# VectorE makes the low halves of the attention's x ahead of the FFN's output addition, and tiles 4 to 7 share one series of inverse deviations

## What is computed

```
def _layernorm(x, axis=-1, eps=1e-05):
    m = jnp.mean(x, axis=axis, keepdims=True)
    v = jnp.var(x, axis=axis, keepdims=True)
    return (x - m) / jnp.sqrt(v + eps)
...
    x = x + 0.5 * _L0_ffn_ref(_layernorm(x, axis=-1), ...)
    x = x + _L0_attn_ref(_layernorm(x, axis=-1), ...)
    x = x + 0.5 * _L0_ffn_ref(_layernorm(x, axis=-1), ...)
```

## Time and profile before

| | |
|---|---|
| median of 3 runs | 733.87 us (733.69 to 734.22) |
| the profiled execution | 733.68 us |
| its span, first to last instruction | 732.0 us |
| PE busy | 713.9 us (98%) |
| DVE, ACT, POOL busy | 523.8, 422.3, 400.6 us (72, 58, 55%) |

### The profile page before, as it was taken

One profiled execution on the slowest core, in us unless ns is written; L12 is line 12 of the kernel. 1 busy time (PEld: TensorE's weight loads), 2 busy tenths in 40 slices (PEclk: granted clock), 3 DMA queues, 4 the chain that ended last, 5 costly groups with the idle time before them and its releaser, 6 DMA issues.

```text
span 732.0 us, 13725 instructions
## 1 busy us (share of the span) xinstructions
PE 713.9 (98%) x3692; PEld 601.6 (82%) x3692; DVE 523.8 (72%) x1773; ACT 422.3 (58%) x1144; POOL 400.6 (55%) x503
## 2 busy tenths in 40 slices
PE   8998989999999999999999999999999999999998
PEld 6786768888888888888888888888888888878776
DVE  6769676767776777677776777667767777778675
ACT  3455675556664775567655765576556665655330
POOL 2566676535853486447743865277535853473420
PEclk9999999999999999999999999999999999999999
DMA  8140003000310022002200220012000300030002
GB/s 268 50 173 30 0 27 105 14 1 2 104 42 2 0 84 59 1 1 72 72 0 1 68 61 15 1 48 82 15 1 13 103 14 1 0 117 1 1 30 87
DMA packets 25868, 32.33 MB, mean 44 GB/s; under 512 B 5833, under 2 KB 14281, under 8 KB 25298
## 3 DMA queue, kind: packets, MB, share of 16 engines
q1 hardware_dynamic: 25232, 30.69, 13.3%
q10 hardware_dynamic: 578, 1.05, 0.4%
HBM read 27.54 MB, written 4.19 MB: 43 GB/s over the span
## 4 chain that ended last, share of the span: by engine, by line
PE 85%; DVE 7%; POOL 4%; ACT 2%; issue 1%; DMA 1%; SPq 0%; DVEq 0%; ACTq 0%; POOLq 0%
PE bank L1157 33%; PE bank L1215 23%; PE bank L1200 8%; PE bank L1179 7%; PE bank L1123 4%; PE bank L1187 4%; PE bank L1176 2%; POOL wo_lo L387 1%; DVE stats L762 1%; PE bank L1166 1%; PE bank L1177 1%; DVE xnT_lo L785 1%; PE bank L1140 1%; DMA x<-in_L_attn_x 1%; PE bank L1108 1%
## 5 line engine op out<-in xcount | busy, mean ns | idle before, releaser
L395 POOL TENSOR_TENSOR swap<-swap,rope 128x512 f32<-128x512 f32 x80 | 104.8, 1309 | 112.2 <-ACT swap L567 112.0
L402 POOL TENSOR_SCALAR_AFFINE_SELECT pT_hi_lo<-pT_hi_lo 128x256 fp32r<-128x256 f32 x128 | 51.9, 406 | 146.1 <-DVE pT_hi_lo L915 146.1
L593 ACT ACTIVATE bank<-sm,nmax 128x128 f32<-128x128 f32 x128 | 47.6, 372 | 111.0 <-DVE nmax L900 110.8
L567 ACT ACTIVATE swap<-bank 64x512 f32<-64x512 f32 x160 | 94.8, 593 | 12.7 <-PE bank L1157 10.2
L601 ACT ACTIVATE pT_hi_lo<-bank 128x256 fp32r<-128x256 f32 x128 | 49.0, 383 | 91.4 <-PE bank L1187 63.0
L915 DVE TENSOR_TENSOR pT_hi_lo<-bank,pT_hi_lo 128x256 fp32r<-128x256 f32 x128 | 53.6, 419 | 50.2 <-ACT pT_hi_lo L601 50.1
L412 POOL TENSOR_TENSOR q_lo<-rot,q_hi 128x512 fp32r<-128x512 f32 x64 | 82.6, 1290 | 1.6 <-ACT q_hi L575 1.6
L1215 PE MATMUL bank<-wo_hi,oT_hi 128*128 128x512 f32 x256 | 74.6, 413 | 0.3 <-DVE x L928 0.3
L1157 PE MATMUL bank<-xnT_lo,wq_hi 128*128 128x512 f32 x256 | 73.3, 390 | 0.0
L1157 PE MATMUL bank<-xnT_hi,wq_hi 128*128 128x512 f32 x256 | 71.9, 393 | 0.8 <-DVE v_lo L886 0.8
L1157 PE MATMUL bank<-xnT_hi,wq_lo 128*128 128x512 f32 x256 | 72.2, 394 | 0.0
(11 more groups left out here) (152 smaller groups left out, 1696.0 us busy)
## 6 DMA issues: line engine op xcount, KB each, us to landing
raw<-in_L_attn_wq SPq DMA_DIRECT2D x32, 256.0 KB, 3.0
raw<-in_L_attn_wo SPq DMA_DIRECT2D x32, 256.0 KB, 2.6
x<-in_L_attn_x SPq DMA_DIRECT2D x4, 512.0 KB, 7.4
raw<-in_L_attn_wk SPq DMA_DIRECT2D x8, 256.0 KB, 2.7
raw<-in_L_attn_wv SPq DMA_DIRECT2D x8, 256.0 KB, 3.5
out<-x SPq DMA_DIRECT2D x8, 256.0 KB, 2.0
raw<-in_L_ffn_W_base ACTq DMA_DIRECT2D x4, 256.0 KB, 5.4
wb_keep_hi<-q_hi SPq DMA_DIRECT2D x1, 1024.0 KB, 5.0
```

What stands on the lines that cost most here:

```text
L395: nc.gpsimd.tensor_tensor(w, w, tab, ALU.mult).then_inc(t2_done, 1)
L402: nc.gpsimd.affine_select(pT_both[:, :, 2, h, :], pT_both[:, :, 1, h, :].bitcast(F32), pattern=[[0, 2], [1, P]], compare_op=ALU.is_ge, fil ...
L567: last = nc.scalar.activation(swap[a:a + half, m % 2, :], A[m % 2][b:b + half, :], ACT.Copy)
```

## The change

VectorE's list: after the last `router`, `x_lo` of tiles 0 and 1 goes ahead of `ffn_out(0, 2)`, and `ht_lo(0, 3)` and `x_lo` of tiles 2 and 3 go ahead of the statistics of tile 5. The deviations of tiles 4 to 7 come from one series on VectorE, four columns wide, with the cosines of the key put between its first and second Newton step. GpSimd's series for tiles 4 and 5 goes (17 rows of its list, `shift` and the guess included), and one `split_lo` moves behind two bias additions. ScalarE's list: two swapped copies before it waits for the series, and all four `xn` of tiles 4 to 7 after. TensorE projects 36 products before it transposes tiles 4 and 5, 12 more before tiles 6 and 7, and puts the first scores ahead of the value pass. No data and no shapes change beyond that.

```diff
@@ rstd_steps @@
-            for _ in range(NEWTON):
+            for n in range(NEWTON):
+                if n == 1 and amid is not None:
+                    amid()
@@ gpsimd @@
             bias(0, 5)
-            split_lo(KT, KT % RING, wq_s[0][:, KT - 1, :], wq_s[1][:, KT - 1, :])
             bias(0, 6)
             bias(0, 7)
-            norm_rstd(1, 4, 6)
+            split_lo(KT, KT % RING, wq_s[0][:, KT - 1, :], wq_s[1][:, KT - 1, :])
             split_lo(5, 0, wv_s[0][:, :, :], wv_s[1][:, :, :])
@@ scalar @@
-            act.wait_ge(rstd_done, 5)
+            act.wait_ge(kept, 32)
+            rope_swap(0, 0)
+            rope_swap(0, 1)
+            act.wait_ge(shift_done, 1)
             xn(1, 4)
             xn(1, 5)
-            act.wait_ge(kept, 32)
-            rope_swap(0, 0)
+            rope_hi(0, 0, 0)
+            rope_swap(0, 2)
             x_hi(1, 4)
             x_hi(1, 5)
-            act.wait_ge(shift_done, 1)
+            rope_hi(0, 1, 0)
             xn(1, 6)
             xn(1, 7)
...
@@ vector @@
+            router(0, NT // 2 - 1)
+            x_lo(1, 0)
+            x_lo(1, 1)
+            ffn_out(0, NT // 2 - 2)
+            norm_stats(1, 4)
+            ht_lo(0, NT // 2 - 1)
             x_lo(1, 2)
             x_lo(1, 3)
+            norm_stats(1, 5)
             ffn_out(0, NT // 2 - 1)
             norm_stats(1, NT - 2)
             norm_stats(1, NT - 1)
-            norm_rstd(1, 6, NT)
             dve.wait_ge(tables_landed, 32)
-            rope_cos(0, 0)
+            norm_rstd(1, 4, NT, lambda: rope_cos(0, 0))
+            rope_cos(0, 1)
             rope_sum(0, 0)
+            rope_sum(0, 1)
+            rope_cos(0, 2)
             x_lo(1, 4)
             x_lo(1, 5)
...
             rope_cos(0, 4)
+            softmax_min(0, 0)
             v_diff(0)
             rope_sum(0, 4)
-            softmax_min(0, 0)
@@ tensor @@
-            project(0, 0, 0, 12, 0)
+            project(0, 0, 0, 36, 0)
             x_transpose(1, 4)
             x_transpose(1, 5)
-            project(0, 0, 12, 36, 0)
+            project(0, 0, 36, 48, 0)
             pe.wait_ge(x_out, 6)
             x_transpose(1, 6)
             x_transpose(1, 7)
-            project(0, 0, 36, 72, 0)
+            project(0, 0, 48, 60, 0)
             scores(0, 0, 0, 0)
+            project(0, 0, 60, 72, 0)
```

More of the change, by code:

```diff
@@ L259, in wo_lo, with rstd_steps @@
             return 10 * g + 7 + i
-        def rstd_steps(engine, then, t0, t1):
+        def rstd_steps(engine, then, t0, t1, amid=None):
             vr, y, a, b = var[:, t0:t1], rstd[:, t0:t1], nt1[:, t0:t1], nt2[:, t0:t1]
@@ L629, in group @@
                             act.wait_ge(vt_done, 2 * KV)
-                            act.wait_ge(rstd_done, 6)
+                            act.wait_ge(rstd_done, 5)
                             xn(2, 0)
@@ L636, in group @@
                         if last and hf == 1 and s == 7:
-                            act.wait_ge(rstd_done, 7)
+                            act.wait_ge(rstd_done, 6)
                             xn(2, 2)
@@ L695, in _ @@
             x_hi(1, 3)
-            act.wait_ge(rstd_done, 5)
+            act.wait_ge(kept, 32)
+            rope_swap(0, 0)
+            rope_swap(0, 1)
+            act.wait_ge(shift_done, 1)
             xn(1, 4)
             xn(1, 5)
-            act.wait_ge(kept, 32)
-            rope_swap(0, 0)
+            rope_hi(0, 0, 0)
+            rope_swap(0, 2)
             x_hi(1, 4)
             x_hi(1, 5)
-            act.wait_ge(shift_done, 1)
+            rope_hi(0, 1, 0)
             xn(1, 6)
             xn(1, 7)
[L707 to L710, removed]
+            rope_swap(0, 3)
+            rope_hi(0, 2, 0)
             x_hi(1, 6)
             x_hi(1, 7)
-            rope_swap(0, 3)
-            rope_hi(0, 2, 0)
             rope_swap(0, 4)
@@ L763, in norm_stats, with norm_rstd @@
                 nc.vector.bn_aggr(mv[:, t, :], stats[:, t, :]).then_inc(aggr, 1)
-            def norm_rstd(ln, t0, t1):
+            def norm_rstd(ln, t0, t1, amid=None):
                 dve.wait_ge(aggr, NT * ln + t1)
-                rstd_steps(nc.vector, then, t0, t1)
+                rstd_steps(nc.vector, then, t0, t1, amid)
                 if ln:
@@ L988, in _ @@
             norm_stats(0, 7)
-            for pr in range(1, NT // 2):
+            for pr in range(1, NT // 2 - 1):
                 router(0, pr)
@@ L992, in _ @@
                 norm_stats(1, 2 * pr - 2)
[L993 to L997, removed]
-                ht_lo(0, pr)
-                if pr < NT // 2 - 1:
-                    norm_stats(1, 2 * pr - 1)
+                x_lo(0, 2 * pr + 2)
+                x_lo(0, 2 * pr + 3)
+                ht_lo(0, pr)
+                norm_stats(1, 2 * pr - 1)
+            router(0, NT // 2 - 1)
[4 more added lines that the diff above has]
+            ht_lo(0, NT // 2 - 1)
             x_lo(1, 2)
             x_lo(1, 3)
+            norm_stats(1, 5)
             ffn_out(0, NT // 2 - 1)
@@ L1005, in _ @@
             norm_stats(1, NT - 1)
-            norm_rstd(1, 6, NT)
             dve.wait_ge(tables_landed, 32)
-            rope_cos(0, 0)
+            norm_rstd(1, 4, NT, lambda: rope_cos(0, 0))
+            rope_cos(0, 1)
             rope_sum(0, 0)
+            rope_sum(0, 1)
+            rope_cos(0, 2)
             x_lo(1, 4)
             x_lo(1, 5)
-            rope_cos(0, 1)
-            rope_sum(0, 1)
-            rope_cos(0, 2)
             rope_sum(0, 2)
+            rope_cos(0, 3)
             x_lo(1, 6)
             x_lo(1, 7)
-            rope_cos(0, 3)
             rope_sum(0, 3)
             rope_cos(0, 4)
+            softmax_min(0, 0)
             v_diff(0)
             rope_sum(0, 4)
-            softmax_min(0, 0)
             group(0, True, False)
```

## The result

The changed kernel takes **734.99 us** (median of 19, 734.68 to 735.5), the kernel before 734.0 us (median of 19) beside it: ratio 1.0014, 95% interval 1.0008 to 1.0021. I had forecast 732.65 us and a range up to 733.8. So the time lies above the range and on the other side of no change: a loss of 1.0 us where a gain of 1.2 was worked out. The profiled execution took 735.5 us, the longest of the 19, so its rows show somewhat more loss than the median has.

The account below looks back on a forecast made before the run. TensorE was taken to bound the kernel: 2.0 us won at the projection's start, 0.77 given back to new waits, 1.23 net, giving 732.65 us against the median; range 731.1 to 733.8, called "same" at 0.63.

Parts of the forecast that it names:

- What bounds the kernel: TensorE, 85% of the chain, busy throughout 130 to 640 us; only its idle times at 55 to 81 us can shrink.
- Part 4: Remaining edits (GpSimd's series removed, weight split moved, softmax minima, semaphore counts): taken as 0, bound 0.3 us either way.
- Part 1: VectorE's order at the FFN's end: projection starts at 58.41 instead of 60.41, 2.0 us won.
- Part 2: VectorE's series starts at 61.97, is held twice by GpSimd; TensorE waits 0.84 us before m = 2.
- both holds: GpSimd's two sine products stop VectorE's series, in the first Newton step until 63.90 and near its end until 66.62.
- the first rival: Series slips past GpSimd's first product by a 0.16 us margin; G 2.6 us earlier, 731.3 us; chance 0.23.
- G: Start of the first projection of `group`, 81.42 us before; forecast 80.19, 1.23 us earlier, and the end moving with it.
- Part 3: ScalarE becomes the chain from `shift` to tile 6, transposed at 72.89; m = 4 at 74.01, G at 80.19.
- The rival of the clock: TensorE's clock drops after four waits within 16 us; one pass at half speed gives 735.4 us; chance 0.05, other losses included.
- The "wrong if": Prediction wrong if G moves and the end does not, or G moves over 1.8 us with both holds in the trace.

Follow-up runs that it names:

- e3: The changed kernel with four more VectorE instructions (fulfilled waits) ahead of the loop, so that it starts at the border, number 441: 732.23 us, ratio 0.9973.
- e5: e3 with GpSimd's first two sine products cut to 4 of 256 columns, leaving the first key's and query's rotation incomplete: 730.63 us, ratio 0.9957.
- e1: The kernel before with one more VectorE instruction, a long fulfilled wait, ahead of the loop: 736.41 us, ratio 1.0029.
- e4: The kernel before with five more VectorE instructions (fulfilled waits) ahead of the loop, so that it starts at the border: 733.79 us, ratio 0.9996.
- e7: The kernel before, loop placed as in e4, with only VectorE's new order at the FFN's end: 735.05 us, ratio 1.0013.
- 438: Placement with 438 VectorE instructions ahead of the loop: the changed kernel there (e3) 732.23 us, the kernel before (e4) 733.79 us.
- e10: The changed kernel with three more VectorE instructions (fulfilled waits) ahead of the loop: 739.44 us, ratio 1.0075.
- e6: e3 with two waits on GpSimd: first sine product after the key's cosines, second after `shift`: 731.61 us, ratio 0.9968; again 731.69 us.
- e11: e6 with GpSimd's second sine product waiting for VectorE's first sum (the rotated key) instead of the series' end: 731.48 us, ratio 0.9966.

## Why the prediction was wrong

- **What bounds the kernel: the step that failed.** "The loop over the heads has nothing to give, the change does not touch it, and whatever is won or lost before it moves the end one for one." The source of the loop is the same and TensorE is full in it, but VectorE's code for it had moved by one instruction. The standstill after each jump, 1.0 to 1.2 us in the trace of before with no product of TensorE waiting for it, moved ahead of the addition and grew to 1.6 to 1.8 us, and TensorE then waited in each pass: 2.84 us lost in five jumps, 1.19 won. That is 1.65 of loss at the last pass; the spans of the two profiled executions differ by 1.8, the medians by 1.0.
- **Part 4, the rest at 0.** It took the changed semaphore counts at 0 because they name the same events, and no term stood for the instructions that waits are: there is one more on VectorE ahead of the loop. The bound was 0.3 us for all of it, and 2.84 were lost.
- **Part 1** was right: the low-rank product at 57.03 (worked out 56.92), the projection at 58.53 (58.41).
- **Part 2** was right: series at 62.18 (61.97), product at 62.89 (62.61), both holds, 0.74 us ahead of m = 2 (0.84), `shift` done at 67.26 (67.05). The margin against the first rival was 0.09 us (62.98 against 62.89) and 0.04 in e3 (62.89 against 62.85), where 0.16 was worked out: that the first hold came was a near thing. Without both holds (e5) G is 3.1 us earlier than before; the rival, with part of a hold left, had 2.6.
- **Part 3** was right: tile 6 at 72.99 (72.89), m = 4 at 74.06 (74.01), G at 80.23 (80.19). The split of the waits was off: 0.15 and 0.70 us where 0.4 and 1 were named, with no effect on the sum. That G was met within 0.04 us is partly luck: ScalarE's chain began 0.22 us late (67.30 against 67.08) and ran 0.16 us shorter.
- **The rival of the clock** was placed on the wrong side. The changed kernel's clock was 1.00 in all stretches read; it is the kernel before with one and with five instructions more (e1, e4), and the first half alone (e7), whose profiles show it fall behind idle times. That belongs to the change's credit; whether it is the 0.3 us by which the gain between medians at 438 (1.56 us) exceeds 1.2 wasn't settled.
- **The "wrong if"** named it: G moved and the end did not. My rivals all lay between 55 and 81 us, so my range had no case for a loss behind G.

The row that could have warned me was in the trace of before: `rinv` with "1.00 <-issue" five times, once for each jump, 5.3 us in all. I had passed over it as idle time of an engine off the path. And the lists of instructions can be counted before any run.

## What to carry over

Where a kernel has a loop with a long list of instructions (301 on VectorE here), count the instructions ahead of it on each engine, waits included, and look for a standstill without a releaser that comes once for each jump; an edit far ahead of the loop can move it on to the path, and a few fulfilled waits can move it off. Judge an edit at equal placement, or its sign may be the placement's. A product on GpSimd that started inside a chain of small VectorE operations cost the chain 1.15 to 1.26 us here, nearly its whole length of 1.29; a wait that starts it behind the chain can be the cheaper one.

## What the runs showed of the hardware

- **Code loads at a jump back.** With the loop's start 4 instructions ahead of the border (the changed kernel) or one ahead (e10), VectorE stood still for 2.5 to 2.6 us at the jump and 2.1 to 2.25 us more at number 441; started at the border (e3), the same loop of 301 instructions made no instruction transfer in a pass. The Trainium skill, "Runtime: NRT & Kernel Launch", section "Instruction fetch mechanics", says that code is fetched in blocks of 256 instructions into a buffer of two, and that a taken branch out of them stalls until the target's block is fetched. The traces agree with the stall and with the count: 301 instructions fit into two such blocks from a border on, and need three from just ahead of it, and the loads are there in the second case alone. They don't show the block's size, and the transfers speak for a smaller one: the packets are of 8192 bytes, by estimate 128 of the built program's instructions of 64 bytes, and the changed kernel's five in a pass start one by one, the last two (264.9, 299.8 us) within 0.7 us of where VectorE reaches the numbers 569 (265.5) and 697 (299.1), which are 128 and 256 behind 441. Only the border at 441 was located by experiment.
- **A fulfilled wait is not free** by its place: one instruction on VectorE ahead of the loop cost 2.2 us (e1), and e10 and e3, which are one apart, differ by 7.5 by their ratios.
- **The hold of a small operation by GpSimd** lasted to the end of GpSimd's whole instruction (1.13 to 1.26 us in the traces of before, after, e3, e6 and e11), also for operations four columns wide.
- **TensorE's clock** fell to 0.50 behind idle times of 1.29 and 0.41 us in the profile of e4, and of 1.31 and 0.41 us in that of e1, and stayed at 1.00 behind 1.34 and 0.41 us in that of before: the same gaps don't always do it. Behind 3.15 us in one piece it fell in the profile of e7, and 10 of its 11 runs have the mean clock of that one, 0.998.
